# Two attention layers on one core: pair-wise rows for the rotary exchange, and zero-padded low keys for the first-half score units

## The reference

```
x = x + L1_attn(layernorm(x)) + L1_ffn(layernorm(x))

q, k, v = split(xn @ w_qkv.T)        # 32 query heads, 4 key/value heads, 64 wide
rope(x) = [x1*cos - x2*sin, x2*cos + x1*sin]   # x1, x2: first and second 32 of a head
scores  = rope(q) . rope(k) / 8, causal over 256 positions
out     = softmax(scores) @ v @ w_o.T
```

## Time and profile before

| | us |
|---|---|
| median of 3 runs | 387.08 |
| lowest, highest | 385.42, 404.5 |
| the profiled execution | 387.23 |
| its span, first to last instruction | 385.4 |
| PE, DVE, POOL, ACT busy | 369.0, 307.1, 279.4, 250.0 |

### The profile page before, as it was taken

How to read it: one execution, slowest core, us unless ns; L and a number is a source line. 1 busy time by engine, 2 the same in 40 slices (tenths; PEclk the granted TensorE clock), 3 DMA queues, 4 the chain that set the end, 5 groups by cost and what they waited for, 6 DMA issues and landing times.

```text
span 385.4 us, 8456 instructions
## 1 busy us (share of the span) xinstructions
PE 369.0 (96%) x2888; PEld 343.6 (89%) x2888; DVE 307.1 (80%) x684; ACT 250.0 (65%) x804; POOL 279.4 (72%) x238
## 2 busy tenths in 40 slices
PE   8998889989999998999999999999999999999995
PEld 3667779979899997999999999999999999998985
DVE  6878999876999885779777888787788879788882
ACT  1368855573987764667667676757666667767671
POOL 3437759789999996977779897667997777776000
PEclk9999999999999999899999999999999999999999
DMA  7996112513444345443345643334565343333300
GB/s 261 414 408 284 27 30 55 138 43 81 110 99 96 79 108 130 112 109 80 87 110 120 157 110 92 93 92 98 131 149 142 93 104 83 84 83 86 79 2 27
DMA packets 34219, 45.15 MB, mean 117 GB/s; under 512 B 5505, under 2 KB 25986, under 8 KB 33794
## 3 DMA queue, kind: packets, MB, share of 16 engines
q1 hardware_dynamic: 34032, 44.62, 43.1%
q10 hardware_dynamic: 146, 0.00, 0.0%
HBM read 13.14 MB, written 1.05 MB: 37 GB/s over the span
## 4 chain that ended last, share of the span: by engine, by line
PE 67%; POOL 15%; DVE 9%; SPq 3%; DMA 2%; ACT 2%; issue 2%; POOLq 0%
PE bank L1287 14%; PE bank L1250 11%; PE bank L1307 10%; PE bank L1004 10%; PE bank L1200 10%; PE bank L1253 3%; POOL woT_lo L606 3%; POOL rope_a L669 2%; POOL split_lo L670 2%; POOL split_hi L668 2%; POOL rope_b L660 2%; PE bank L1013 2%; DMA wq0T<-in_L_attn_w_qkv_dram 2%; PE bank L1159 2%; POOL rope_a L658 2%
## 5 line engine op out<-in xcount | busy, mean ns | idle before, releaser
L515 ACT ACTIVATE bank<-bank,neg_max 128x256 f32<-128x256 f32 (+1 forms) x256 | 101.3, 397 | 10.0 <-DVE neg_max L911 9.9
L524 ACT ACTIVATE probT_hi<-bank 128x512 fp32r<-128x512 f32 x96 | 57.6, 600 | 73.6 <-PE bank L1004 73.4
L911 DVE TENSOR_REDUCE neg_max<-bank 128x2 f32<-128x512 f32 (+1 forms) x96 | 65.9, 687 | 31.2 <-PE bank L1253 30.9
L1287 PE MATMUL bank<-probT_hi,v 128*128 128x256 f32 x384 | 76.4, 295 | 0.6 <-DVE oT_lo L939 0.6
L660 POOL TENSOR_TENSOR rope_b<-turned,cst 128x512 f32<-128x512 f32 x36 | 47.1, 1308 | 40.6 <-DMA turned<-raw 40.6
L1250 PE MATMUL bank<-kT,qT 128*128 128x256 f32 (+1 forms) x512 | 73.4, 276 | 1.7 <-DMA qT<-split_lo 1.7
L927 DVE TENSOR_TENSOR prob<-bank,rsum 128x512 f32<-128x512 f32 x96 | 66.4, 691 | 3.3
L1250 PEld LDWEIGHTS bank<-kT,qT 128*128 128x128 f32 x512 | 66.5, 191 | 1.9 <-DMA qT<-split_lo 1.9
L933 DVE TENSOR_TENSOR probT_lo<-bank,probT_hi 128x512 fp32r<-128x512 f32 x96 | 65.4, 681 | 0.5 <-ACT probT_hi L524 0.4
L1287 PEld LDWEIGHTS bank<-probT_hi,v 128*128 128x128 f32 x384 | 58.6, 189 | 3.5 <-issue 2.2
L1004 PE MATMUL bank<-cst,prob 128*128 128x128 f32 x384 | 58.4, 275 | 2.2 <-DVE prob L927 2.2
(11 more groups left out here) (158 smaller groups left out, 735.2 us busy)
## 6 DMA issues: line engine op xcount, KB each, us to landing
turned<-raw SPq DMA_DIRECT2D x144, 64.0 KB, 2.0
qT<-split_hi SPq DMA_DIRECT2D x64, 128.0 KB, 2.4
qT<-split_lo SPq DMA_DIRECT2D x64, 128.0 KB, 2.4
wq0T<-in_L_attn_w_qkv_dram SPq DMA_DIRECT2D x4, 512.0 KB, 7.9
wout<-in_L_attn_w_out_dram SPq DMA_DIRECT2D x4, 512.0 KB, 12.4
nat_qkv<-in_L_attn_w_qkv_dram SPq DMA_DIRECT2D x2, 1024.0 KB, 20.5
nat_o<-in_L_attn_w_o_dram SPq DMA_DIRECT2D x1, 2048.0 KB, 21.4
kT<-split_hi SPq DMA_DIRECT2D x16, 128.0 KB, 2.4
```

Source lines behind the costliest of these rows:

```text
L515: ins = nc.scalar.activation(own, own, ACT.Exp, bias=neg_max[it % 2][:, first + j:first + j + 1], accum_out=sums[it % 2][:, first + j:firs ...
L524: nc.scalar.activation(probT[0][:, n % 4, :], bank[2 + n % 2][:, :], ACT.Copy).then_inc(t_hi, 1)
L911: dve.tensor_reduce(neg_max[n // UNITS % 2][:, unit_columns(n % UNITS)], score_bank(n)[:, :].rearrange("p (h k) -> p h k", h=heads), AX.X, ...
L1287: ins = pe.matmul(group_bank(), v[b % 2][:, DH * z:DH * z + P], p, start=m == 0, stop=m == last)
```

## The change

Four things are changed.

1. **Rows side by side.** The rows of `w_qkv` that make queries and keys are reordered on the host, so that the two entries which rotate together lie in neighbouring partitions (`pairs`). The tables of cosines and sines follow. The exchange is then between even and odd partitions: two DMAs of 64 partitions with stride 2 in place of four of 32 (L356 of the changed kernel).
2. **First-half units.** POOL writes the high part of a query block into its own tile `q_hi`, where 128 partitions hold two heads; it stays there while its iteration runs. `k_pad` holds for each key head the low keys of the first 128 positions twice: once in partitions 0 to 63 with zeros below (`z` = 0), once in 64 to 127 with zeros above (`z` = 1). One matmul of `q_hi` with 256 columns of `k_pad` adds high by low for two heads at once. A first-half unit so has 4 matmuls with 128 columns and 2 with 256. Low by low is no longer added there. Each key block gets 4 more DMAs, 12 in all, and POOL clears the zero parts once (`pad`).
3. **POOL's order.** `weights_lo` takes one unit after each of blocks 4 to 11, in place of two after each of 4 to 7. Each block's first product waits for the low part of the block before (`split_done`), since `rope_a` and `rope_b` now have one buffer.
4. **Memory.** `oT`, `split_hi`, `rope_a`, `rope_b` have one buffer in place of two, some tiles lie elsewhere, and one copy on ACT (`ones_r`) comes later.

```diff
-    ang = np.arange(SEQ, dtype=np.float32)[None] * np.tile(inv, P // inv.size)[:, None]
-    sign = np.where(np.arange(P) % DH < DH // 2, np.float32(-1), np.float32(1))[:, None]
+    ang = np.arange(SEQ, dtype=np.float32)[None] * np.tile(np.repeat(inv, 2), P // DH)[:, None]
+    sign = np.where(np.arange(P) % 2, np.float32(1), np.float32(-1))[:, None]
...
-        oT = [[at(f"oT{i}_{w}", k * K + 4 * K * j, [P, 4, SEQ], F32R) for j, w in enumerate(("hi", "lo"))]
-              for i, k in enumerate((148, 64))]
+        oT = [at(f"oT_{w}", (148 + 4 * j) * K, [P, 4, SEQ], F32R) for j, w in enumerate(("hi", "lo"))]
+        q_hi = [at(f"q_hi{i}", k * K, [P, HG // 2, SEQ], F32R) for i, k in enumerate((168, 104))]
+        k_pad = [at(f"k_pad{i}", k * K, [P, HKV, 2, P], F32R) for i, k in enumerate((184, 108))]
...
-        probT = [at(f"probT_{w}", k * K, [P, 4, 512], F32R) for w, k in (("hi", 104), ("lo", 112))]
+        probT = [at(f"probT_{w}", k * K, [P, 4, 512], F32R) for w, k in (("hi", 64), ("lo", 112))]
...
-        split = [at(f"split_{w}", 156 * K + 4 * K * i, [P, 2, 2, SEQ], F32R) for i, w in enumerate(("hi", "lo"))]
-
-        rope_a = at("rope_a", 164 * K, [P, 2, 512])
-        rope_b = at("rope_b", 168 * K, [P, 2, 512])
+        split_hi = at("split_hi", 156 * K, [P, 2, SEQ], F32R)
+        split_lo = at("split_lo", 158 * K, [P, 2, 2, SEQ], F32R)
+        rope_a = at("rope_a", 164 * K, [P, 2, SEQ])
+        rope_b = at("rope_b", 166 * K, [P, 2, SEQ])
...
-        ones_r = at("ones_r", 185 * K, [P, P], F32R)
-        wcol = at("wcol", 186 * K, [P, DIM])
-        idle_in = at("idle_in", 187 * K, [P, 512], BF16)
+        ones_r = at("ones_r", 162 * K, [P, P], F32R)
+        wcol = at("wcol", 163 * K, [P, DIM])
+        idle_in = at("idle_in", 136 * K, [P, 512], BF16)
...
-            return 8 if BLOCKS[n][0] == "k" else 4
+            return 12 if BLOCKS[n][0] == "k" else 4
...
-            return [w[:, j:j + 2, P * c:P * c + P] for w in oT[it % 2]]
+            return [w[:, j:j + 2, P * c:P * c + P] for w in oT]
...
-                d = DH // 2
-                for at_row in range(0, P, DH):
-                    lower, upper = slice(at_row, at_row + d), slice(at_row + d, at_row + DH)
-                    sp.dma_start(turned[lower, n % 2, :], raw[upper, n % 2, :]).then_inc(turn_landed[n % 2], 16)
-                    sp.dma_start(turned[upper, n % 2, :], raw[lower, n % 2, :]).then_inc(turn_landed[n % 2], 16)
+                for h in range(2):
+                    sp.dma_start(turned[h:P:2, n % 2, :], raw[1 - h:P:2, n % 2, :]).then_inc(turn_landed[n % 2], 16)
...
                 for w in range(2):
-                    for s in range(2):
-                        src = split[s][DH * w:DH * w + DH, n % 2, :, :].bitcast(F32)
+                    own = slice(DH * w, DH * w + DH)
+                    low = split_lo[own, n % 2, :, :].bitcast(F32)
+                    if what == "q":
+                        high = q_hi[it % 2][own, 2 * half:2 * half + 2, :].bitcast(F32)
+                    else:
+                        high = split_hi[own, :, :].bitcast(F32)
+                    for s, src in enumerate((high, low)):
                         if what == "q":
                             sp.dma_start(qT[it % 2][DH * s:DH * s + DH, 4 * half + w:4 * half + 4:2, :].bitcast(F32), src).then_inc(placed[n % 2], 16)
                         else:
                             for z in range(2):
                                 sp.dma_start(kT[b % 2][DH * z:DH * z + DH, w:HKV:2, s, :].bitcast(F32), src).then_inc(placed[n % 2], 16)
+                    if what == "k":
+                        for z in range(2):
+                            sp.dma_start(k_pad[b % 2][DH * z:DH * z + DH, w:HKV:2, z, :].bitcast(F32), low[:, :, 0:P]).then_inc(placed[n % 2], 16)
...
-            act.wait_ge(ld["cst"], 16)
-            nc.scalar.activation(ones_r[:, :], cst[:, C_ONE:C_ONE + P], ACT.Copy).then_inc(ones_done, 1)
...
+                if step == WCOL_STEP - 2:
+                    act.wait_ge(ld["cst"], 16)
+                    act.wait_ge(lo0_done, B)
+                    nc.scalar.activation(ones_r[:, :], cst[:, C_ONE:C_ONE + P], ACT.Copy).then_inc(ones_done, 1)
...
+            def pad(i):
+
+                for z in range(2):
+                    own = k_pad[i][DH * (1 - z):DH * (1 - z) + DH, :, z, :]
+                    pool.memset(own.bitcast(F32), 0.0).then_inc(pad_zero, 1)
+                    pool.wait_ge(pad_zero, 2 * i + z + 1)
+
+            pool.wait_ge(v_zero, 2)
+            pool.wait_ge(blk_done, 1)
+            pad(0)
...
-                whole, half, a, z = (t[:, n % 2, :].rearrange("p (j t) -> p j t", j=2) for t in (raw, turned, rope_a, rope_b))
+                whole, half = (t[:, n % 2, :].rearrange("p (j t) -> p j t", j=2) for t in (raw, turned))
                 pool.wait_ge(raw_done, n + 1)
-                pool.tensor_tensor(a, whole, cos, ALU.mult)
-                pool.wait_ge(turn_landed[n % 2], 64 * (n // 2 + 1))
-                own_done(pool.tensor_tensor(z, half, sin, ALU.mult))
+                if n:
+                    pool.wait_ge(split_done, n)
+                pool.tensor_tensor(rope_a[:, :, :], whole, cos, ALU.mult)
+                pool.wait_ge(turn_landed[n % 2], 32 * (n // 2 + 1))
+                own_done(pool.tensor_tensor(rope_b[:, :, :], half, sin, ALU.mult))
 
             def rope_sums(n):
 
                 if n >= 2:
                     has_landed(pool, n - 2)
-                a, z = (t[:, n % 2, :].rearrange("p (j t) -> p j t", j=2) for t in (rope_a, rope_b))
-                hi, lo = (t[:, n % 2, :, :] for t in split)
+                a, z, lo = rope_a[:, :, :], rope_b[:, :, :], split_lo[:, n % 2, :, :]
+                if BLOCKS[n][0] == "k":
+                    hi = split_hi[:, :, :]
+                else:
+                    _, it, part = BLOCKS[n]
+                    hi = q_hi[it % 2][:, 2 * part:2 * part + 2, :]
+                    if it >= 2:
+                        pool.wait_ge(s_full, (it - 2) * UNITS + 3 + part)
                 pool.tensor_tensor(hi, a, z, ALU.add)
                 own_done(pool.tensor_tensor(a, a, z, ALU.add))
                 pool.tensor_tensor(lo, a, hi.bitcast(F32), ALU.subtract).then_inc(split_done, 1)
...
             weights_lo(7, 8)
             tile_root(7)
+            pool.wait_ge(root_out, TILES + B + 2)
+            pad(1)
             rope_products(3)
             rope_sums(3)
             weights_lo(8, 10)
             for n in range(4, len(BLOCKS)):
                 rope_products(n)
                 rope_sums(n)
-                weights_lo(2 * n + 2, min(2 * n + 4, len(W_UNITS)))
+                weights_lo(min(n + 6, len(W_UNITS)), min(n + 7, len(W_UNITS)))
...
                 c, heads, h, keys = unit_heads(u)
+                if c == 0 and n < HKV * UNITS * 2:
+                    pe.wait_ge(pad_zero, 2 * (b + 1))
                 for j in range(heads):
-                    for s in range(2):
+                    for s in range(c + 1):
                         pe.matmul(ps[:, keys * j:keys * j + keys], qT[it % 2][:, h + j, P * c:P * c + P], kT[b % 2][:, g, s, 0:keys],
                                   start=j == 0 and s == 0, stop=False, skip_group_check=True)
+                    if c == 0 and j % 2:
+                        pe.matmul(ps[:, keys * (j - 1):keys * (j + 1)], q_hi[it % 2][:, (h + j) // 2, 0:P], k_pad[b % 2][:, g, :, :],
+                                  start=False, stop=False, skip_group_check=True)
                 diag = ps[:, :].rearrange("p (h k) -> p h k", h=heads)[:, :, P * c:P * c + P]
...
-                            ins = pe.matmul(bank[BANK_OUT][:, DIM * e:DIM * e + DIM], oT[it % 2][s][:, j, e:e + 2 * P - 1:2],
+                            ins = pe.matmul(bank[BANK_OUT][:, DIM * e:DIM * e + DIM], oT[s][:, j, e:e + 2 * P - 1:2],
...
+    if name == "L1_attn_w_qkv":
+        turned = (H + HKV) * DH
+        pairs = a[:turned].reshape(-1, 2, DH // 2, a.shape[-1]).swapaxes(1, 2).reshape(turned, -1)
+        return by_rows(np.concatenate([pairs, a[turned:]]).T)
+    if name in ("L1_attn_w_o", "L1_ffn_w_fc", "L1_ffn_w_proj", "L0_ffn_weight", "L0_attn_w_qkv"):
```

More of the change, by code:

```diff
@@ L193, in build @@
         out_full, out_added = sem("out_full"), sem("out_added")
-        v_zero = sem("v_zero")
+        v_zero, pad_zero = sem("v_zero"), sem("pad_zero")
         raw_done, rope_done, split_done = sem("raw_done"), sem("rope_done"), sem("split_done")
@@ L1356, in by_rows @@
         return w.reshape(-1, P, w.shape[-1]).transpose(1, 0, 2)
-    if name in ("L1_attn_w_qkv", "L1_attn_w_o", "L1_ffn_w_fc", "L1_ffn_w_proj", "L0_ffn_weight", "L0_attn_w_qkv"):
+    if name == "L1_attn_w_qkv":
[3 more added lines that the diff above has]
+    if name in ("L1_attn_w_o", "L1_ffn_w_fc", "L1_ffn_w_proj", "L0_ffn_weight", "L0_attn_w_qkv"):
         return by_rows(a.T)
```

## The result

| | before, us | after, us |
|---|---|---|
| median of 4 runs | 387.16 | 381.25 |
| lowest, highest | 385.42, 404.5 | 380.05, 381.45 |
| profiled execution, its span | 387.23, 385.4 | 380.05, 378.2 |
| mean granted clock of it | 0.996 | 0.999 |

The changed kernel takes 0.9855 of the time, with a 95% interval of 0.9825 to 0.9884 (one run of before, 404.5 us, is over 4% above the others and left out of the ratio). That is faster by more than the measurement is uncertain and by less than 2%. The forecast was 378.8 in a range of 377.0 to 383.0: the median of 381.25 is 2.4 above it and lies in the range.

The account below looks back on a forecast made before the run. PE's program was taken to set the pace, with one PE wait and low clock in iteration 3. The sum was 387.23 - 4.8 (first-half units) - 3.6 (wait and clock) = 378.8 us, range 377.0 to 383.0.

Parts of the forecast that it names:

- Both terms of the sum: First-half units gain 4.8 us over 26 units; the vanished PE wait in iteration 3 and its low clock gain 3.6 us.
- the wait at (3, 3): Iteration 3, unit 3: PE's 1.71 us wait for a low query part goes; rival that it stays, 382.4 us, chance 0.15.
- 4 x 0.105 + 2 x 0.119 = 0.66, so 0.185 us less: First-half unit on PE: four 128-column and two 256-column matmuls, each at its own pace, 0.66 us instead of 0.84.
- the units gain little: Rival, first-half units: 256-column matmuls hold all six to 0.119 us, saving 0.13 per unit; 380.3 us, chance 0.12.
- 2 of 4 count: Last two iterations: only two of four first-half units gain, as the chain passes unit 2's scores, then ACT and DVE.
- 134 to 135.5: Sign on SP's queue: block 8's first placing comes at 134 to 135.5 us.
- my 1.3 to 2.1: Iteration 3, unit 3: the margin in us by which PE's wait for the low query part was forecast to go.
- POOL waits for it, PE does not: nil: Exchange: two 128 KB DMAs for four of 64 finish 0.9 us sooner, but gain nothing in the sum.
- the step on SP's list: SP's queue after block 8: 12 placings and 2 exchange DMAs, 14 x 0.66 = 9.2 us, ending at 143.7.
- the issue of 1.72: SP's queue before the change: one drawn-out issue of 1.72 us, used for the wait term's lower bound of nil.
- The wait at (7, 3): Iteration 7, unit 3: possible wait in the rival "slower" (389.6 us, chance 0.03); the forecast had 4.6 us of cover.
- my line at 379.3: Whole kernel: time dividing over 2% faster (7.7 us) from no change; chance of faster 0.52.

Follow-up runs that it names:

- the 4.17 us wait: Changed kernel with POOL's old order (two weight units after each of blocks 4 to 7): 386.58 us (10 runs), ratio 1.0007; PE waits 4.17 us at iteration 3, unit 3.

## Why the prediction was right, and what it had wrong

Both terms of the sum have the cause that the prediction gave. With the old matmuls put back, the 0.32 us per iteration go. With the old order put back, the wait at (3, 3) and the low clock return. The sum came out 1.2 us too much against the profiled execution.

**The units: the mechanism right, the size 0.6 us too large.** The step "4 x 0.105 + 2 x 0.119 = 0.66, so 0.185 us less" measured 0.68 and 0.16. In iterations 2 to 13 that makes 12 x 0.32 = 3.84 us in place of 4.44. The old matmuls put back give the same 3.8 there. 0.68 lies between my 0.66 and the 0.71 of the rival "the units gain little"; the matmul between others of another width does not keep exactly the pace of its own row. The estimate by the Trainium skill's page TensorE: Matmul & The Clock Gate, "Back-to-back issue gap", was 0.13 us per unit. The trace shows 0.16, between that and my 0.185; the absolute times of the estimate (a unit of 0.52 us) lie below the measured 0.68.

**"2 of 4 count" held, but the end of the program took the gain back.** From the mask of unit 0 of iteration 14 to the end of the span nothing is gained: 42.98 us before and 43.00 after. That stretch has to be split at its last instructions. Timelines of PE, DVE and SP, first of the kernel before, then of the changed one:

```profile
342.42 0.28 PE L1253 MATMUL bank<-mask_b,ident_b 128*128 128x256 bf16 x1
...
382.31 0.69 DVE L946 TENSOR_TENSOR x<-x,bank 128x512 f32<-128x512 f32 x1 [1.81 <-PE bank L1307]
383.02 0.34 SPq L393 DMA_DIRECT2D out_dram<-x  x1
```

```profile
335.20 0.28 PE L1287 MATMUL bank<-mask_b,ident_b 128*128 128x256 bf16 x1
...
374.78 0.69 DVE L975 TENSOR_TENSOR x<-x,bank 128x512 f32<-128x512 f32 x1 [1.81 <-PE bank L1341]
375.50 0.34 SPq L399 DMA_DIRECT2D out_dram<-x  x1
```

From the mask to the last addition on DVE it is 39.89 us before and 39.58 after: 0.31 less, which is two units of 0.16, one in each iteration. The chain goes through the scores of unit 2 and then through ACT and DVE, as I read from the earlier trace rows. The other two units gain nothing: PE waits for `prob` there, 1.7 us in two waits where it was 1.4. From the issue of the last store to the end of the span it is 2.4 us before and 2.7 after. All nine traces of kernels built on the changed one show these 2.7 us, that with the old matmuls too; the kernels with the order alone and with the exchange alone show 2.4. SP goes on 2.02 us after the issue in all of them, and the 0.29 us lie behind it, on POOL, between its last two semaphore events (0.08 us before, 0.37 after). The prediction has no term for that, and which part of the change brings it stays open. The four units of iterations 0 and 1 gained nothing, as said (34.50 us for the two, before 34.44).

**The wait and the clock: right in the profiled execution.** They gave 3.54 us against 3.6. The steps: block 8 done at 135.0 (134.5, and "134 to 135.5" for its placing), 14 issues until the end of the exchange at 144.15 (143.7), block 9's last part landing at 149.0 (148.1), PE there at 150.2. One issue of 0.97 and half a microsecond of POOL made the difference; the margin of 1.2 us is just under my 1.3 to 2.1.

**But half of that term is not in every execution.** The 41 executions of the kernel before that were timed beside the experiments form three groups by their mean clock: 18 at 0.998 to 1.000 (384.93 to 385.79 us), 15 at 0.995 or 0.996 (386.08 to 387.54) and 8 at 0.991 (387.92 to 388.97). The profiled one, at 0.996, is like the second group. All should have the wait, by the order of their instructions; the clock's fall after it, 1.9 us, only a part has. The times fit two falls, each there or not: 385.2 us with neither, 386.4 with the one in the start-up (1.2), 387.1 with the one after the wait (1.9), 388.3 with both. In the second group three executions lie at 386.1 to 386.4 and twelve at 386.8 to 387.5, and the mean of the third is 388.3. By that count 20 of the 41 have the fall after the wait. Those of the first group against those of the changed kernel at 1.000 give 385.2 - 379.9 = 5.3 us, which is 3.84 and 1.5 for the wait alone. The order alone and the exchange alone, at 0.998 or more, have medians of 383.9 and 384.0, 1.3 and 1.2 below the same 385.2. I infer all this from the times; only one execution of before has a trace. So it was luck that the execution which I took as the base had the fall: against one at 1.000 the forecast of 3.6 us would have been more than twice what came. With the 4.17 us wait all of ten executions showed a clock of 0.996 or less.

**"POOL waits for it, PE does not: nil" failed as a step, though not in the sum.** Alone the exchange brings 386.8 - 384.3 = 2.5 us, nearly all that the order brings alone (2.9). PE does not wait for the exchange, but what PE waits for is issued behind the exchange of block 10 on SP's queue. With 14 issues I had counted two fewer there, 1.3 us, in the step on SP's list, and never asked what they would do by themselves; and the issue of 1.72 went too, though one of 1.34 among the placings of block 9 came in. The last part is issued 150.02 - 148.17 = 1.85 us sooner, more than the wait of 1.71 if all else stays.

**The rest.** `oT`, `pad`, `ones_r` and the late weight units, taken together, cost no more than the 0.3 us at the end: the old matmuls put back leave a kernel of 382.1 us of span, beside 382.0 for the order alone and 382.0 for the exchange alone. DVE is busy 82.05 of 100 us from 240 to 340, and PE waits for nothing in that stretch. The wait at (7, 3) did not come.

**The sum.** 387.23 - 7.18 = 380.05: of the 1.2 us too much, 0.6 are the units' size in iterations 2 to 13, 0.1 the same in the last two, 0.3 the end of the program, 0.1 the wait, and 0.1 the start-up with the first two iterations. The median of the four runs is another 1.2 higher. Three of them had a mean clock of 0.995 or 0.996, and by their times I put that down to the fall in the start-up; none of the three has a trace. Ten later runs of the same kernel had a median of 379.8 to 379.9. The chance for "faster by over 2%" was too high for the same reasons: my line at 379.3 was only 0.5 from a forecast whose terms were all taken at their full value.

## What to carry to other kernels

Two edits that take away the same wait do not add up: try each by itself, and ask of a third one (here the moves into `k_pad`) how much of that margin it eats. Where a mean clock differs between executions of one kernel, compare those of the same mean clock before a term is read off, and price a wait by itself and the clock's fall after it by how often it comes. Where a gain seems missing from a stretch at the end of a program, split the stretch at its last instructions before you blame the chain: here the gain was there, and 0.3 us behind the last store hid it.

## What the runs showed that I had not expected

- A matmul of 256 columns between pairs of 128 takes 0.17 us, as does each pair of 128: six take 0.68, where the rows of before give 0.105 and 0.119 each. Grouped, the four of 128 take 0.39 and the two of 256 take 0.28.
- The span ends 2.7 us after the issue of the last store in the changed kernel and 2.4 us after it in the kernel before, though SP goes on after 2.02 us in both.
- An exchange of every second of 128 partitions, 128 KB, lands in 2.0 us, no later than one of 32 neighbouring partitions with 64 KB, while other moves of 128 KB take 2.4.
- The same idle pieces of PE, 3.6 us busy of 5, are followed by a clock of 0.77 over five us in one execution and of 1.00 in another. Of ten executions of the kernel whose trace has a wait of 4.17 us none had a mean clock above 0.996; of 41 of the kernel whose trace has one of 1.71 us, 18 had 0.998 or more.
